# Turning the router's tiles by a transposing DMA within SBUF instead of TensorE, ScalarE and VectorE

## The reference, cut to what matters

```
x = x + gnn(layernorm(x))        # gnn: h = x W^T + b, then a degree-weighted sum over edges
flat = layernorm(x)              # what the router and the experts read
logits = flat @ router_w.T + router_b            # 8 experts
topk_vals, topk_idx = top_k(logits, 2)
topk_w = softmax(topk_vals)
out = sum over e of topk_w[e] * (gelu(flat @ w1[e].T + b1[e]) @ w2[e].T + b2[e])
x = x + layernorm(out + flat) * ln_w + ln_b
```

## Time and profile before

| what | value |
|---|---|
| median of 3 runs | 656.46 us (655.33 to 658.19) |
| profiled execution, its own time | 656.9 us |
| span of its trace | 654.8 us |
| outside the span | 2.1 us |
| TensorE busy with matmuls | 559.6 us (85%) |
| VectorE busy | 487.1 us (74%) |
| ScalarE busy | 247.8 us (38%) |
| GpSimd busy | 207.7 us (32%) |
| mean granted TensorE clock | 0.939 |

### The profile page before, as it was taken

How to read it: one execution, slowest core, us unless ns; L and a number is a source line. 1 busy time by engine, 2 the same in 40 slices (tenths; PEclk the granted TensorE clock), 3 DMA queues, 4 the chain that set the end, 5 groups by cost and what they waited for, 6 DMA issues and landing times.

```text
span 654.8 us, 12794 instructions
## 1 busy us (share of the span) xinstructions
PE 559.6 (85%) x3848; PEld 311.5 (48%) x3849; DVE 487.1 (74%) x1301; ACT 247.8 (38%) x374; POOL 207.7 (32%) x200
## 2 busy tenths in 40 slices
PE   1598999989989999999485999999999999999300
PEld 0243455545544455555374465656565655555100
DVE  8998967786614678889887677877786868574297
ACT  4333333323325224344452334343434343321380
POOL 2740000000000025565755353535353535141131
PEclk9989999999999999999778899999999999999755
DMA  5694000000000823444656496969696969364879
GB/s 208 210 376 194 3 2 2 2 2 3 2 2 13 330 108 135 152 167 152 201 135 228 140 280 198 259 222 242 237 252 224 240 233 242 125 103 129 224 233 276
DMA packets 35052, 106.16 MB, mean 162 GB/s; under 512 B 8978, under 2 KB 9391, under 8 KB 34992
## 3 DMA queue, kind: packets, MB, share of 16 engines
q1 hardware_dynamic: 24912, 73.86, 30.3%
q0 software_dynamic: 8896, 27.38, 20.1%
q10 hardware_dynamic: 1184, 4.20, 1.9%
HBM read 71.75 MB, written 33.67 MB: 161 GB/s over the span
## 4 chain that ended last, share of the span: by engine, by line
PE 70%; DVE 16%; DMA 5%; issue 4%; ACT 2%; DVEq 1%; POOL 1%; POOLq 0%; SPq 0%; ACTq 0%
PE ps L1864 6%; PE ps L1747 6%; PE ps L1748 6%; PE ps L1865 6%; PE ps L1866 6%; PE ps L1843 5%; PE ps L1845 5%; PE ps L1844 5%; PE ps L1671 4%; PE ps L1672 4%; PE ps L1673 4%; PE ps L1825 3%; PE ps L1617 3%; PE ps L1598 2%; DVE oh_all L1028 2%
## 5 line engine op out<-in xcount | busy, mean ns | idle before, releaser
L513 POOL TENSOR_TENSOR work<-work 128x1024 f16<-128x1024 f32 x9 | 19.2, 2131 | 222.4 <-ACT work L872 222.4
L606 POOL DMA_INDIRECT acc_rows<-work,ids_out x24 | 52.2, 2177 | 107.1 <-DVE work L1472 107.1
L1747 PE MATMUL ps<-wbufs,rows_and_counts 128*128 128x512 f16 x200 | 75.8, 379 | 0.5 <-DVE wbufs L1252 0.5
L1748 PE MATMUL ps<-wbufs,rows_and_counts 128*128 128x512 f16 x200 | 75.8, 379 | 0.0
L1843 PE MATMUL ps<-rows_and_counts,wbufs 128*128 128x336 f16 (+2 forms) x256 | 74.8, 298 | 0.8 <-DVE rows_and_counts L1410 0.8
L1864 PE MATMUL ps<-wbufs,rows_and_counts 128*128 x192 | 73.8, 384 | 1.7 <-issue 1.3
L1845 PE MATMUL ps<-rows_and_counts,wbufs 128*128 128x336 f16 (+2 forms) x256 | 74.8, 298 | 0.0
L1844 PE MATMUL ps<-rows_and_counts,wbufs 128*128 128x336 f16 (+2 forms) x256 | 74.8, 298 | 0.0
L1425 DVE SCALAR_TENSOR_TENSOR wbufs<-stage,wbufs 128x1024 f16<-128x1024 f32 x56 | 67.2, 1219 | 10.2 <-ACT wbufs L899 9.6
L1865 PE MATMUL ps<-wbufs,rows_and_counts 128*128 x192 | 73.8, 384 | 0.0
L1866 PE MATMUL ps<-wbufs,rows_and_counts 128*128 x192 | 73.7, 384 | 0.0
(11 more groups left out here) (305 smaller groups left out, 1105.0 us busy)
## 6 DMA issues: line engine op xcount, KB each, us to landing
stage<-wst_in SPq DMA_DIRECT2D x72, 512.0 KB, 6.2
acc_rows<-work SPq DMA_DIRECT2D x10, 512.0 KB
x_rows<-work SPq DMA_DIRECT2D x10, 512.0 KB
t<-x_in SPq DMA_DIRECT2D x1, 4096.0 KB, 14.1
wbufs<-b_in ACTq DMA_DIRECT2D x8, 512.0 KB
wbufs<-acc_rows SPq DMA_DIRECT2D x8, 512.0 KB, 6.2
t<-x_in SPq DMA_DIRECT2D x1, 3072.0 KB, 10.1
t<-x_in SPq DMA_DIRECT2D x1, 2048.0 KB, 7.7
```

The lines of the kernel that those rows point to most:

```text
L1747: mm(o, ct_hi[:, cs], hs[:, at:at + HALF], start=(m == 0), stop=False, skip_group_check=True)
L1748: mm(o, ct_hi[:, cs], hs[:, D + at:D + at + HALF], start=False, stop=False, skip_group_check=True)
```

## The change

`turn2`, its PSUM tile, ScalarE's copy and VectorE's subtraction are gone. SyncE issues one transposing DMA for each tile, from `xs` to `x2t`, between the two stores. It carries both halves: 128 rows of 2048 float16 numbers, 512 KB, in 16 blocks of 128x128. SyncE waits for `router_done` of the tile before, as `x2t` is a single buffer. TensorE's `route` waits for the DMA, and ScalarE waits for it before it writes the next `xs`.

```
@@ SyncE
                 sp.dma_start(acc_rows[rows, :], xn).then_inc(x2_stored, 16)
                 sp.wait_ge(xs_done, NT + r + 1)
+                sp.wait_ge(router_done, r)
+                sp.dma_start_transpose(x2t.rearrange("p (b k) -> p b k", k=P), xs).then_inc(x2t_in, 16)
                 sp.dma_start(x2_rows[rows, :], xs.bitcast(F32)).then_inc(x2_first_stored if r < FIRST_TILES else x2_stored, 16)
@@ ScalarE
-            for r in range(NT + 1):
-                if r >= 1:
-                    act.wait_ge(x2t_done, r)
-                    act.wait_ge(router_done, r - 1)
-                    a.activation(x2t[:, 0:D], x2t_ps, ACT.Copy).then_inc(x2t_hi_done, 1)
-                if r < NT:
-                    sqrt_var(r)
-                    act.wait_ge(xn_done, NT + r + 1)
-                    act.wait_ge(x2t_done, r)
-                    stored(act, r)
-                    a.activation(xs[:, 0:D], xn, ACT.Copy).then_inc(xs_hi_done, 1)
+            for r in range(NT):
+                sqrt_var(r)
+                act.wait_ge(xn_done, NT + r + 1)
+                act.wait_ge(x2t_in, 16 * r)
+                stored(act, r)
+                a.activation(xs[:, 0:D], xn, ACT.Copy).then_inc(xs_hi_done, 1)
@@ VectorE
-            def x2t_lo(r):
-                dve.wait_ge(x2t_hi_done, r + 1)
-                v.tensor_tensor(x2t[:, D:], x2t_ps, x2t[:, 0:D], ALU.subtract).then_inc(x2t_lo_done, 1)
...
-                if 1 <= r < NT - 1:
-                    x2t_lo(r - 1)
...
                 if r == NT - 1:
-                    x2t_lo(r - 1)
...
-                if r == NT:
-                    x2t_lo(r - 1)
@@ TensorE
-            def turn2(r):
-                pe.wait_ge(xs_done, NT + r + 1)
-                pe.wait_ge(x2t_lo_done, r)
-                transposed(x2t_ps, xs).then_inc(x2t_done, 1)
-
             def route(r):
-                pe.wait_ge(x2t_lo_done, r + 1)
+                pe.wait_ge(x2t_in, 16 * r + 16)
...
-                if 1 <= r <= NT:
-                    turn2(r - 1)
```

More of the change, by code:

```diff
@@ L307, in build @@
         agg_ps = [bank(0, 2), bank(2, 2)]
-        x2t_ps = bank(4, 2)
         router_ps = bank(6)
@@ L407, in build @@
         x2_stored = sem("x2_stored")
-        x2t_done = sem("x2t_done")
-        x2t_hi_done = sem("x2t_hi_done")
-        x2t_lo_done = sem("x2t_lo_done")
+        x2t_in = sem("x2t_in")
         x4_done = sem("x4_done")
```

## The result

| | before | after |
|---|---|---|
| median | 656.44 us (655.33 to 658.19) | 663.1 us (660.95 to 664.13, 4 runs) |
| ratio, 95% interval | | 1.0086 (1.0067 to 1.0104) |
| profiled execution, its own time | 656.9 us | 660.95 us |
| span | 654.8 us | 659.2 us |

The change makes the kernel 0.9% slower, some 6 us. I had forecast slower, but by 21.5 us. The profiled execution of after is the fastest of its four, so what it shows of the loss, 4 us, is the low end.

What follows compares the result with a forecast made beforehand. TensorE was taken to bound the aggregation, and after the change the `xs` store queued behind the transfer. Intervals +20.2 us and tail +0.6 made +21 on 656.5: 677, stated as 678 us, range 648 to 735.

Steps and rivals of the forecast that it cites:

- pricing it at nothing: Aggregation: should TensorE's clock fall in its 2.9 us of idle time per tile, no loss of time was counted.
- 7.1 foreseen: Aggregation: eight turns of 0.89 us leave TensorE's path, 7.1 us in all.
- the 9.46 us: Aggregation: TensorE's period per tile without its turn, 10.35 - 0.89 us.
- The first of the four loops: Aggregation: `xs` store queued behind the transfer delays VectorE's next `xn`; binds from X = 3.05 on.
- X: Each tile: time the transfer keeps DMA engines or SyncE from the store behind it; taken as 6.0 us.
- the 20.2: Aggregation: nine intervals of 12.4 us, 111.6 us together instead of 91.4, so +20.2 us.
- X + 6.4: Aggregation: period from store landing 2.2 + X after `xs` is ready, then 4.12 us for `xn` and `xs`, plus gaps.
- +0.6 us: Tail: turned tile 9 arrives 6.9 us after `xs` is ready; `choose(9)` starts at 328.9 instead of 328.28.
- Cheap and hidden: Rival, aggregation: X at most 3, TensorE stays the bound at 9.46 us; 648.6 us; chance 0.34.
- Blocks one after another: Rival, transfer: 16 blocks in a row take 27 us, period 33.6 us, time 890 us; chance 0.17.
- The costs balance: Rival, aggregation: X between 3.5 and 4.2, or only the second loop binds; 657 us; chance 0.11.
- the dear case: Likeliest case, aggregation: X between 4.2 and 9, time 660 to 707 us; chance 0.38.

Runs made afterwards that it cites:

- the last experiment: Changed kernel with transfer in two halves, VectorE waiting only for the store that reads `xn`, last tile turned by TensorE: 650.88 us, 0.9917.
- xn_own_store: Changed kernel, with VectorE waiting before `xn` only for the store that reads `xn`, not for that of `xs`: 655.84 us, 0.9975.
- after_again: The changed kernel unaltered, measured once more beside the other runs: 664.85 us, 1.0149.
- last_by_pe: Changed kernel, with the last tile turned by TensorE, ScalarE and VectorE as before the change: 660.27 us, 1.0057.
- store_first: Changed kernel, with SyncE issuing the store of `xs` ahead of the transposing transfer: 664.99 us, 1.0134.
- alone: Kernel before, plus unused transposes, a store and transpose-store pairs in a stage with idle DMA engines: 657.95 us (before 656.97).
- beside: Kernel before, plus eight unused transposes in an idle stage, alone or beside GpSimd's scatters, most coming after the data: 656.02 us (before 657.42).
- beside_earlier: Kernel before, plus eight unused transposes in an idle stage, alone or beside GpSimd's scatters, those issued sooner: 658.82 us (before 657.38).
- copies5: Kernel before, with five more 512 KB stores of `xs` ahead of its store, ScalarE waiting for them too: 705.19 us, 1.0748.
- scatter_late: Changed kernel, with GpSimd's scatter of token numbers moved behind its splitting of the weights' piece: 667.13 us, 1.0162.

## Why the prediction was wrong in size and right in kind

**The mechanism** came as it was put. L1598, L866's copy from PSUM and L1268 are gone from the stage; VectorE waits before `xn` for the DMA to x_rows; TensorE is below full; its clock stayed at 1.00, so pricing it at nothing was right. TensorE's busy time fell by 6.4 us (7.1 foreseen), and the 9.46 us came out in the last experiment as 9.42. The first of the four loops bound: all nine later `xn` waited for the store, and without that wait the intervals fell to 85.9 (*xn_own_store*).

**The step that failed is the size of X.** I took 6.0 us, "the upper part" of 1.35 to 7.9, because a transposed row is nearer to short pieces than to 4 KB rows. It measured 2.9 to 3.4 us in the seven ordinary tiles, 4.4 in the two with a stall, and 3.4 on average. Its parts: data of 2.5 to 2.7 us, about twice a copy's; a lag of 1.2 us in place of 0.8; and SyncE held for 2 us by the issue, hidden under these two. Nine times (3.4 - 6.0) is -23 us, more than the 20.2 that I had for the intervals. The choice by likeness had no number behind it, and likeness to the copy would have been the better one: 3.4 lies nearer to 1.35 than to 7.9.

**A second term was too small,** and hid part of this. I took the store's landing for the end of its data, 2.2 us after issue; it is 2.65. With that and the gaps the period is X + 7.0, not X + 6.4, so nine intervals are 5 us longer than my rule gives: -23 and +5 leave +2.2 of the +20.2. With X right and the rule as it stood, I would have said 9.8 us a tile, 3 us less than before in nine intervals, and so a gain instead of the loss. That the sign came out right is in part luck.

**The tail was mis-sized the other way.** I had +0.6 us, with the last transfer landing 6.9 us after issue; it took 8.8 (12.1 in *after_again*), and from the last `xn` to the experts' first matmul the loss was 2.9 us. My sum gave the last transfer the same X as all others, though the earlier trace rows showed the DMA engines busier there, 0.67. They are at 0.92 now, with gathers, a piece of the weights and the store of `xs` in the same microseconds. That this is why it lands late is argued, not shown. That the tail's loss hangs on this transfer is shown, by *last_by_pe*.

**The rivals.** "Cheap and hidden" fell, though X came close to it: it asked for X of at most 3, and even in the tiles with X = 2.9 VectorE waited for the store, since with X + 7.0 the loop binds from 2.5 on. The Trainium skill ("DMA: Bandwidth & Descriptors", Latency and other measured facts) gives 261 GB/s for a non-contiguous case and 350 to 400 for a contiguous one; the trace shows about 200 in the stage and 206 to 219 by itself, so the Trainium skill's lower figure is some 25% above what was measured here, and the estimate X = 2.0 also leaves out the longer lag. "Blocks one after another" fell too: the Trainium skill ("VectorE: DVE Perf Modes", The three transpose paths) has 1309 ns for one block, while 16 blocks took 2.5 us of data in one transfer. "The costs balance" is what happened in the intervals, with +2.2 us, but by way of the longer landing and not of its X of 3.5 to 4.2. Its 657 us left out the tail's 3 us. So the time, 663.1, fell into the dear case's own range of 660 to 707, while X stayed below that case's 4.2: that is luck, too.

**What I had not seen** was how little stood between loss and gain. I called VectorE's wait in `stored` the thing on which the forecast rests, and did not ask whether it needs to be there. It waits for a store of `xs`, which it does not touch. With that wait off, and the last tile left to TensorE, the same transfers make the kernel 0.6% faster; in two halves, 0.8%.

**Open.** What stops a transfer for 0.5 to 1.5 us with nothing beside it, why the fifth and the eighth tile are the long ones, why the last transfer takes 8.8 to 12.1 us, and how large the loss is between 0.9% and 1.5%.

## What to carry to other kernels

Before you put a transfer into a queue, list what is issued behind it and which engine waits for each of those: the transfer's price is paid there, at the first buffer that is not yet free, and not where its own result is used. Look then at what each of these waits really protects; one that covers more than its own buffer costs nothing until something slow moves in ahead. And price the last tile of a loop by itself, since nothing hides it: there the old way may be kept.

## What the runs showed of the hardware that I had not expected

- The transposing transfer of 512 KB within SBUF moved about 200 GB/s in a busy stage and 206 to 219 in an idle one; stores of the same size moved 410.
- Its issue held SyncE for 1.3 to 2.1 us in after, where an ordinary one takes 0.32, and for 3.3 to 5.4 us right behind a store (*store_first*). The store issued behind it held SyncE for another 0.95 to 1.4 us and, in the tail, 2.73.
- A store of 512 KB landed 2.65 us after its issue, some 0.5 us after the end of its data (*alone*).
- Now and then a transfer stopped for 0.5 to 1.5 us, with nothing beside it (*beside*, *beside_earlier*).
- Six stores of 512 KB, issued back to back, moved at 400 GB/s, 1.3 us each; in one tile the last packets then took 2 us more (*copies5*).
- Two VectorE operations on 8 columns took 2.19 us beside GpSimd's back-to-back tensor operations (*scatter_late*), and 0.43 us in after, with no tensor operation of GpSimd beside them.
